# A transformer layer on one core: the loads and the clock at the start, the place of one small matmul, and the place of the first scan

## The reference

```
x = x + cross_attention(layernorm(x), ctx, mask, Wq, Wkv, Wproj, bproj)   # 16 heads of 16
x = x + mamba(layernorm(x), ...)     # own norm, in_proj, causal conv of 4 taps, silu,
                                     # h = exp(delta*A)*h + delta*B*x over 64 steps, 512 x 16 states,
                                     # y = sum_n h*C + D*x, gated by silu(z), out_proj
x = x + ffn(layernorm(x), w_gate, w_up, w_down)  # weights rounded to -1, 0, 1 times their mean |w|
```

## Time and profile before

| | us |
|---|---|
| three timed runs | 414.05, 415.46, 415.11; median 415.11 |
| profiled execution | 414.41 |
| its span | 412.6 |
| TensorE busy | 357.3 (87%) |
| VectorE busy | 350.4 (85%) |
| GpSimd busy | 280.6 (68%) |
| ScalarE busy | 276.8 (67%) |
| mean granted TensorE clock | 0.991 |

### The profile page before, as it was taken

How to read it: one execution, slowest core, us unless ns; L and a number is a source line. 1 busy time by engine, 2 the same in 40 slices (tenths; PEclk the granted TensorE clock), 3 DMA queues, 4 the chain that set the end, 5 groups by cost and what they waited for, 6 DMA issues and landing times.

```text
span 412.6 us, 8645 instructions
## 1 busy us (share of the span) xinstructions
PE 357.3 (87%) x2864; PEld 241.6 (59%) x2868; DVE 350.4 (85%) x727; ACT 276.8 (67%) x592; POOL 280.6 (68%) x329
## 2 busy tenths in 40 slices
PE   4899999979998999886988899998889778889774
PEld 1566767666766765453555567666666556647442
DVE  1569888777989778958899999989999999988795
ACT  2276599749966993489658679857874554166574
POOL 0055566555647472248987699999999699986830
PEclk9999999999999999998899999999999999999999
DMA  6981011010100000019400000276000000000001
GB/s 203 389 329 53 2 51 41 14 51 3 53 2 0 2 3 0 2 40 259 114 2 0 2 1 29 82 185 143 2 1 2 0 2 0 2 0 2 13 27 64
DMA packets 22623, 22.41 MB, mean 54 GB/s; under 512 B 1042, under 2 KB 20242, under 8 KB 22068
## 3 DMA queue, kind: packets, MB, share of 16 engines
q1 hardware_dynamic: 22020, 21.39, 16.5%
q10 hardware_dynamic: 560, 0.48, 0.4%
HBM read 20.75 MB, written 1.12 MB: 53 GB/s over the span
## 4 chain that ended last, share of the span: by engine, by line
PE 28%; DVE 24%; issue 17%; POOL 16%; ACT 13%; DMA 1%; DVEq 0%; POOLq 0%; PEldq 0%; ACTq 0%
POOL both L1867 12%; DVE both L1573 7%; PE ps L531 7%; PE ps L500 4%; ACT both L1162 3%; PE ps L483 3%; DVE xc L1539 2%; DVE both L1405 2%; PE ps L518 2%; PE ps L561 2%; ACT both L1002 2%; PE ps L548 2%; DVE f_s L1665 1%; ACT both L1148 1%; PE ps L735 1%
## 5 line engine op out<-in xcount | busy, mean ns | idle before, releaser
L1867 POOL TENSOR_TENSOR both<-both 128x1024 f32<-128x1024 f32 x64 | 149.4, 2360 | 8.7 <-DVE both L1573 8.3
L1573 DVE TENSOR_TENSOR_SCAN both<-both,ps 128x1024 f32<-128x1024 f32 x64 | 142.9, 2272 | 6.1 <-PE ps L735 6.0
L1813 POOL TENSOR_SCALAR both<-both,rden 128x256 f32<-128x256 f32 x128 | 61.7, 496 | 61.4 <-DVE rden L1412 61.4
L1162 ACT ACTIVATE both<-delta,a_neg 128x504 f32<-128x504 f32 x120 | 74.9, 704 | 11.2 <-DVE both L1573 11.1
L745 PE MATMUL ps<-con,both 128*128 128x128 f32 x512 | 71.6, 278 | 7.6 <-POOL both L1867 7.5
L1002 ACT ACTIVATE both<-both,negmax 128x256 f32<-128x256 f32 x128 | 63.3, 498 | 16.9 <-DVE negmax L1405 16.9
L745 PEld LDWEIGHTS ps<-con,both 128*128 128x128 f32 x512 | 56.1, 141 | 29.4 <-issue 16.0
L735 PE MATMUL ps<-both 32*128 32x256 f32 x512 | 46.6, 433 | 9.8 <-DVE both L1573 7.3
L1405 DVE CUSTOM_DVE_ANT_0 both<-ps,both 128x256 f32<-128x256 f32 x128 | 46.9, 417 | 6.7 <-PE ps L483 5.5
L531 PE MATMUL ps<-both 128*128 128x512 f32 x64 | 32.8, 637 | 7.4 <-DMA both<-in_ctx_t 6.0
L500 PE MATMUL ps<-con,both 128*128 128x128 f32 x256 | 38.2, 275 | 0.0
(11 more groups left out here) (145 smaller groups left out, 603.8 us busy)
## 6 DMA issues: line engine op xcount, KB each, us to landing
both<-bounce SPq DMA_DIRECT2D x16, 512.0 KB, 5.5
both<-in_ctx_t SPq DMA_DIRECT2D x8, 512.0 KB, 3.7
both<-in_wg SPq DMA_DIRECT2D x1, 1024.0 KB, 8.8
both<-in_wu SPq DMA_DIRECT2D x1, 1024.0 KB, 10.8
both<-in_wd SPq DMA_DIRECT2D x1, 1024.0 KB, 12.6
win_sb<-in_win SPq DMA_DIRECT2D x1, 1024.0 KB, 14.6
resid<-in_x SPq DMA_DIRECT2D x1, 896.0 KB, 6.4
both<-in_wkv SPq DMA_DIRECT2D x1, 512.0 KB, 3.7
```

Of the source, the lines that this page charges most:

```text
L1162: act.activation(da[sl % 2].rearrange("p (a s n t) -> p a s n t", a=GT, n=HN, s=2)[:, :, :, n, 1:L], delta[:, idx % RING_D].rearrange("p ( ...
L1573: dve.tensor_tensor_scan(h_sb[:, hu % RING_H], da[e.slot % 2][:, e.tt * HU:(e.tt + 1) * HU], bank(inflow_bank(hu), 2), 0.0, ALU.mult, ALU. ...
L1813: pool.tensor_scalar(s, s, rden[:, u, q:q + 1], 1.0, ALU.mult, ALU.mult).then_inc(normed, 1)
L1867: pool.tensor_tensor(g_sb[:, hu % RING_G].rearrange("p (n s t) -> p s n t", n=HN, s=2), h_sb[:, hu % RING_H].rearrange("p (s n t) -> p s n ...
```

## The change

Four edits. On SyncE and ScalarE the first loads are cut and put in another order: only the keys' half of Wkv is loaded ahead of the first context tile; Wq (formerly on ScalarE's queue), the values' half of Wkv and the mask of the first tile follow when the keys' half has landed, and the rest of the mask and the remaining loads when the values' half has landed. TensorE runs seven [128 x 128] matmuls of the ones ahead of everything, its own `start` too, and VectorE's memsets and ScalarE's two loads stand ahead of their `start`. The matmul of the weights' sums stands ahead of the next tile's scores. And `scan(0)` stands ahead of `copy_ut(1, 1)` and `u_of(2)`; `u_of(2)` and `u_of(3)` follow scans 1 and 2.

```diff
+WARM = 7
-        N_FIRST, N_LOADED, N_LOADED2 = 16 * 2, 16 * 5, 16 * 3
+        N_FIRST, N_LOADED, N_LOADED2 = 16, 16 * 5, 16 * 3
             start(sp, SP)
-            sp.dma_start(wkv_sb[:], wkv.rearrange("(k p) n -> p k n", p=P)).then_inc(loaded_kv, 16)
+            wkv_rows = wkv.rearrange("(k p) n -> p k n", p=P)
+            sp.dma_start(wkv_sb[:, :, 0:D], wkv_rows[:, :, 0:D]).then_inc(loaded_kv, 16)
...
             load_ctx(Tile(0, 0))
-            sp.wait_ge(loaded_first, N_FIRST)
-            sp.wait_ge(ctx_loaded[0], 16)
-            sp.dma_start(mask_sb[:], mask).then_inc(loaded_mask, 16)
+            sp.wait_ge(loaded_kv, 16)
+            sp.dma_start(wq_sb[:], wq.rearrange("(k p) n -> p k n", p=P)).then_inc(loaded_wq, 16)
+            sp.dma_start(wkv_sb[:, :, D:2 * D], wkv_rows[:, :, D:2 * D]).then_inc(loaded_wv, 16)
+            sp.dma_start(mask_sb[:, 0:TK], mask[:, 0:TK]).then_inc(loaded_mask, 16)
             load_ctx(Tile(0, 1))
+            sp.wait_ge(loaded_wv, 16)
+            sp.dma_start(mask_sb[:, TK:], mask[:, TK:]).then_inc(loaded_masks, 16)
...
         def _(pe):
+            pe.wait_ge(consts, 1)
+            for _ in range(WARM):
+                pe.matmul(bank(7)[:, 0:P], ones[:], ones[:], start=True, stop=True)
             start(pe, PE)
...
                 for u in range(UNITS - 2 if last else UNITS):
+                    if tile.t == W_MEAN and u == 5:
+                        pe.wait_ge(w_abs, count(6))
+                        pe.wait_ge(y1_ready, count(tile.t))
+                        pe.matmul(bank(4)[:, 0:6], ones[:], wsum[:], start=True, stop=True).then_inc(w_sum, 1)
                     if last:
...
                     elif u == PE_FIRST_HALF:
                         scores(nxt, 0, 2 if nxt.last() else 4)
-                    if tile.t == W_MEAN and u == 5:
-
-                        pe.wait_ge(w_abs, count(6))
-                        pe.wait_ge(y1_ready, count(tile.t))
-                        pe.matmul(bank(4)[:, 0:6], ones[:], wsum[:], start=True, stop=True).then_inc(w_sum, 1)
...
             keys(t0, 1)
+            pe.wait_ge(loaded_wq, 16)
             queries(t0)
             scores(t0, 0, 4)
+            pe.wait_ge(loaded_wv, 16)
             vals(t0, 0)
...
-            start(act, ACTE)
             act.dma_start(resid[:, 0], x[0:P]).then_inc(loaded_x, 16)
             act.dma_start(con[:], cons).then_inc(loaded_first, 16)
-            act.dma_start(wq_sb[:], wq.rearrange("(k p) n -> p k n", p=P)).then_inc(loaded_first, 16)
+            start(act, ACTE)
...
-            start(dve, DVE)
-
             dve.memset(ones[:], 1.0).then_inc(consts, 1)
             dve.memset(eps[:], EPS).then_inc(consts, 1)
             dve.memset(neg_half[:], -0.5).then_inc(consts, 1)
             dve.memset(bank(4), 0.0).then_inc(consts, 1)
+            start(dve, DVE)
...
                 dve.wait_ge(masked, count(tile.t * 16 - 16))
+                if tile.t == 1:
+                    dve.wait_ge(loaded_masks, 16)
...
             norm_y1(t7)
-            copy_ut(1, 1)
-            u_of(2)
             for hu in range(NHU):
                 scan(hu)
                 if hu == 0:
+                    copy_ut(1, 1)
                     copy_late_gate()
+                if hu == 1:
+                    u_of(2)
+                if hu == 2:
                     u_of(3)
```

More of the change, by code:

```diff
@@ L262, in build @@
         loaded_mask, loaded_x = sem("loaded_mask"), sem("loaded_x")
+        loaded_masks, loaded_wq, loaded_wv = sem("loaded_masks"), sem("loaded_wq"), sem("loaded_wv")
         loaded = sem("loaded")
```

## The result

| | before | changed |
|---|---|---|
| median of 22 runs | 415.11 us | 414.38 us |
| lowest and highest run | 414.05, 416.06 (22 runs) | 412.01, 415.30 (22 runs) |
| profiled execution | 414.41 us | 413.96 us |
| its span | 412.6 us | 412.2 us |
| mean granted clock | 0.991 | 0.988 |

The ratio is 0.9977, with a 95% interval of 0.9967 to 0.9986, which is 0.6 to 1.4 us faster. The medians differ by 0.7 us, not by the 4.1 us forecast. The interval excludes no change, but the gain is smaller than the 0.3% (1.25 us) that the prediction took as its bound.

A forecast was written before the change was run, and what follows sets the result against it. Bound: the chain ending last, serial for the first 12 us, then through TensorE in attention and VectorE and TensorE in the scans. 1.3 + 1.6 + 0.6 = 3.5 us off 414.41 gives 410.9, plus 0.1: 411.0 us, range 409.4 to 413.9.

The forecast's parts named there:

- the start's clock: At the start: seven matmuls of ones have TensorE's clock up for the keys at 6.1 us; 1.3 us won.
- The loads: At the start: the reordered loads win nothing as such; keys start at 6.1 to 6.2 us, 0.1 to 0.2 us lost.
- rival (c): At the start: TensorE's raising held until the seven matmuls are done, context load late, keys cold; 417.3 us; chance 0.07.
- The loads behind the first ones: At the start: wall, the last, lands at 16.5 to 17.7 us, wanted at 17.4; costs 0 to 0.3 us, 0 taken.
- The means: In attention tile 3: the weights' sums ahead of the scores remove VectorE's 1.57 us wait; 1.6 us won.
- The bound from the beat: In attention: tile 3's beat of 20.60 us less the next tile's 18.96 bounds the means' gain at 1.64 us.
- Rival (b): In attention tile 3: the means' wait is replaced by GpSimd's pace, leaving 0.3 of 1.6 us; 412.2 us; chance 0.10.
- Scan 0: At the first scans: scan 0 earlier starts TensorE's in-flow and scan 4 earlier; 0.6 us won, bounds 0 and 1.0.
- VectorE's own limit: At the first scans: VectorE's copies, u's and scans take 11.7 us from 189.2, allowing scan 4 by 200.9 us.
- a second stretch at 0.50 granted clock: Sign of a wrong forecast: TensorE's clock at its lower level in a second stretch; no place or size given.
- Rival (a): At the start: the ones don't raise the clock for the keys, or it falls before; 0.2 us lost, 412.4 us; chance 0.27.

The follow-up runs named there:

- start alone: The changed kernel with the sums' matmul and scan 0 put back, so only the start's edits against the kernel before: 414.99 us.
- no edits of the start: The kernel before with the weights' sums moved and scan 0 ahead, without any of the start's edits: 414.29 us.
- late block: The changed kernel with the first context load waiting for nothing and its seven matmuls of ones behind the twelfth of TensorE's 27 semaphore raisings: 412.13 us.
- twelve ones: The changed kernel with twelve matmuls of ones in front instead of seven: 412.09 us.
- scan 0 alone: The kernel before with only scan 0 moved ahead of copy_ut(1) and the u's: 415.61 us.
- means alone: The kernel before with only the weights' sums matmul moved ahead of the scores: 414.51 us.
- load freed: The changed kernel with the first context load waiting for no semaphore: 413.84 us.
- ones between: The changed kernel with the first context load unheld and twelve matmuls of ones spread among TensorE's semaphore raisings: 412.37 us; with filler matmuls too, 411.74 us.
- no ones: The changed kernel without its seven matmuls of ones (WARM = 0): 414.38 us.
- filler alone: The changed kernel with twice four idle 128-column matmuls in TensorE's gaps before up(5) and down(2) of the late feed-forward: 413.64 us.

## Why the prediction was wrong

The forecast for the profiled execution was 410.9 us, and it took 413.96. The 3.06 us between them come apart as follows.

**The step that failed is the start's clock: "If the clock is up at 6.1 us, the keys' first half takes 1.9 us ... and I book 1.3."** Booked for the start were 1.3 us won; it lost 0.72 (tile 1's keys at 19.64 us, not 18.92). That is 2.02 of the 3.06 us. The step's own arithmetic held: the ones end at 4.4 us as worked out, the gap of 2 us before the keys was named, and with the clock up the keys took 1.95 us, as worked out. In that profile (start alone, the same text of the start) the term was 0.81 us, since the keys came 0.5 to 0.6 us later than I had them. What was wrong is the choice: that the clock would be up. I had a row for each side, 2.15 us of idleness before a fall and 1.86 us with none, wrote that 2 us lie at the edge, and then gave the case without harm the larger chance. The two rows are of the steady state, in which the clock is already high. The question here was another one, whether it *rises* before the keys, and for that the only row was the start of before, where by the durations the clock rose towards the end of the first keys and not at once. The Trainium skill, "TensorE: Matmul & The Clock Gate", section on what is actually happening, says that the chip looks at activity in windows that run free of the kernel's start. The runs agree with it: with one text of the start the rise came at different moments, inside the first keys in the profile of before (3.42 us), not before the second group in that of no edits of the start (3.75 and 2.19 us). By it seven ones with a gap behind them work in some executions and not in others; that agrees with the keys of 1.95 us in start alone and with one run in 22 of the changed kernel. That a prelude which reaches up to the keys brings the clock up is what the late block shows: 412.13 against 413.84 us.

**The loads** were forecast to lose 0.1 to 0.2 us and lost 0.4. The context load was issued at 1.98 us, earlier than my 2.45: the raising started at 1.1, not 1.6 us, so handing over 28 instructions takes nearly nothing. It took 4.23 us, the upper end of my 3.2 to 4.2, although it had 256 KB less in front of it. The same page's table of the engine gives TensorE a queue of 64; the 28 instructions of seven ones agree with it, but with 48 of twelve ones the raising began at 2.5 us, so here the queue took fewer than 48. The measurement decides: rival (c), the raising held back, is no rival at seven ones and costs 1.4 us of raising at twelve. The loads behind the first ones had their cover, as said: wall was issued at 11.63 us, 0.6 later than I had it, and VectorE's keys and masks ran without a wait for it.

**The means**: 1.6 us forecast, 1.33 to 1.42 measured in the profiles of the kernels that have the edit. The bound from the beat had been 1.64. With the tile's keys 0.71 us later than before (73.83 against 73.12), the matmul comes 1.51 us earlier in its tile (85.97 against 86.77) and the transposes of xn 1.35 us (91.65 against 92.29), which is the term. Tile 3 still takes 19.25 us to tile 4's 18.96, since four small operations of VectorE (86.29 to 87.17 us) are still in it, 0.7 us of which I had called hidden. The scores were not moved back (86.41 against 85.69, so 0.01 us). Rival (b) is refuted.

**Scan 0**: 0.6 us forecast, 0.45 measured, and by another path than I wrote. The in-flow did start early (191.58 us), but from then on VectorE, with three scans, a copy and two products in a row, is what ends last. My estimate of VectorE's own limit (200.9 us, 0.95 us below scan 4's 201.85) counted 0.69 us for the u between scans 1 and 2, whose row has 1.70; why it takes that long there I have not settled, but not because of TensorE's clock, since it took 1.72 us in scan 0 alone too, where the clock didn't fall. That the gain did not come from the clock is shown by scan 0 alone.

**What no step had**: the stretch of low clock in the feed-forward part, 0.65 us in the profile, 1.73 us in that of scan 0 alone. I had listed "a second stretch at 0.50 granted clock" among the signs of being wrong, but looked for it at the scans. It is not caused by one of the edits in any way that I could find: of the 11 profiles without filler it is in six (changed, means alone, scan 0 alone, load freed, seven late, ones between) and not in five (before, start alone, no ones, no edits of the start, twelve ones), with and without the means moved on both sides. How often it is in the other runs can't be read from their mean granted clock, which was 0.988 to 0.991 in the profiles with it and 0.990 to 0.994 in those without. With filler matmuls in the two holes it is in none of three profiles, and the medians are 0.6 to 0.7 us lower in two pairs of kernels (filler alone against changed, and the two with ones between). What decides in which execution the clock falls there is open.

The sum: 2.02 (start) + 0.24 (means) + 0.15 (scan 0) + 0.65 (feed-forward) = 3.06 us. Rival (a), cold keys at 412.4 us, had the mechanism and missed 1.56 us: 0.52 at the start (keys 0.4 us later where it had 0.2, and 3.75 us long where it had the 3.42 of before) and the three others. Also the median: I had taken the profile of before as typical of its start. The three kernels with the same start have profiles in which it took 1.34, 1.46 and 2.09 us more, so that the start in the profile of before was a lucky one, and part of what the means and scan 0 win is missing where their profiles are set against it. That doesn't explain the medians. The means and scan 0 are worth 1.8 us in every profile that has both, and no edits of the start is 1.0 us below the kernel before in the median; the other 0.8 us are not accounted for. The low clock of the last part is the nearest candidate, since with filler the median is 1.4 us below the kernel before, but filler without the start's edits was not run.

The best version measured, with twelve ones between the raisings, the load freed and the filler, takes 411.74 us, 2.6 us below the changed kernel and 3.5 us below the one before. The terms in its profile are 1.22 + 1.39 + 0.42 = 3.03 us. That comes near the 3.5 us that I had expected of the change itself, but with three more edits.

## What to carry to other kernels

A prelude that is to raise TensorE's clock has to last until the work that it is for: here the same seven matmuls were worth nothing 2 us ahead of it and 1.7 us directly ahead of it. Put it behind, or between, whatever else the queue has to do first, since it delays all that stands behind it. And a term that hangs on the clock's moment is a chance and not a size: take it from more than one execution, and look for the other waits of TensorE, anywhere in the program, at which the clock can fall. And look at all runs of a kernel and not at the median alone: a group of long runs can hide what an edit is worth.

## What was not expected of the hardware

- The granted clock's rows say 1.00 for the first microseconds in every profile, although a group of four passes takes 3.75 us there and 1.95 us later. At the start the clock is to be read from durations.
- With 12 matmuls of float32 (24 passes, 24 weight loads) ahead, the next instructions of TensorE's queue began 1.4 us later than with 7 (2.5 against 1.1 us).
- A DMA that is issued earlier need not land so much earlier: 0.64 us at the issue of the first context load became 0.24 us at its landing.
- A low clock over some 6.8 us at the first scans of the changed kernel (worked out from the granted clock of the windows from 188 to 200 us) cost nothing that could be measured, one of some 3.4 us in the feed-forward part 0.65 us. What it costs depends on who ends last there.
